# Attention 1: causal masking of the value-side scores moved from TensorE to GpSimd, and the denominators of the fifth block summed on TensorE

## The reference, cut to what matters

```python
B, L, D, H, HD, LD = 2, 1024, 128, 16, 64, 32
q = einsum('bld,dhk->blhk', x, Wq);  latent = einsum('bld,dc->blc', x, Wkv_down)
k = einsum('blc,chk->blhk', latent, Wk_up);  v = einsum('blc,chk->blhk', latent, Wv_up)
attn = einsum('bqhd,bkhd->bhqk', q, k) / sqrt(HD)
mask = arange(L)[None, :] <= arange(L)[:, None]
attn = softmax(where(mask, attn, neg_inf), axis=-1)
y = einsum('bhqk,bkhd->bqhd', attn, v);  out = x + einsum('bqhd,hdo->bqo', y, Wout)
```

## Time and profile before

| | before |
|---|---|
| median of three runs | 2079.44 us |
| profiled execution, its own time | 2081.13 us |
| its span, first to last instruction | 2079.3 us |
| TensorE busy | 1822.3 us (88%) |
| VectorE (DVE) busy | 1597.8 us (77%) |
| ScalarE (ACT) busy | 1195.2 us (57%) |
| GpSimd (POOL) busy | 952.4 us (46%) |
| mean granted TensorE clock | 0.951 |

### The profile page before, as it was taken

One profiled execution on the slowest core, in us unless ns is written; L12 is line 12 of the kernel. 1 busy time (PEld: TensorE's weight loads), 2 busy tenths in 40 slices (PEclk: granted clock), 3 DMA queues, 4 the chain that ended last, 5 costly groups with the idle time before them and its releaser, 6 DMA issues.

```text
span 2079.3 us, 33170 instructions
## 1 busy us (share of the span) xinstructions
PE 1822.3 (88%) x12499; PEld 1206.6 (58%) x12499; DVE 1597.8 (77%) x2101; ACT 1195.2 (57%) x2056; POOL 952.4 (46%) x384
## 2 busy tenths in 40 slices
PE   6899999986889976999999888899887777999998
PEld 4444454355445665767777555556554555677776
DVE  4566656448779978577776899899999999777666
ACT  2354544533878821546555677777777666555554
POOL 3366556512387822010000288888989899300000
PEclk9799999998999987999999999999999999999999
DMA  3111211000222210001100000000001000101000
GB/s 87 32 32 32 58 32 37 1 12 0 74 81 82 102 36 16 20 32 31 31 16 1 1 2 2 1 1 1 2 1 32 1 2 2 46 16 31 16 16 21
DMA packets 39555, 53.98 MB, mean 26 GB/s; under 512 B 6179, under 2 KB 22790, under 8 KB 39398
## 3 DMA queue, kind: packets, MB, share of 16 engines
q1 hardware_dynamic: 38870, 50.82, 8.6%
q10 hardware_dynamic: 528, 1.05, 0.2%
HBM read 37.83 MB, written 1.18 MB: 19 GB/s over the span
## 4 chain that ended last, share of the span: by engine, by line
PE 53%; DVE 18%; issue 17%; POOL 5%; ACT 4%; DMA 1%; SPq 1%; DVEq 0%; ACTq 0%; POOLq 0%; PEldq 0%
PE ps L46 10%; PE ps L48 8%; PE ps L47 8%; DVE negm L2708 7%; PE ps L1690 5%; PE ps L532 3%; PE ps L548 3%; PE ps L1678 2%; PE ps L581 2%; DVE AF L2715 2%; PE ps L573 2%; POOL AR_plain L2513 1%; PE ps L2537 1%; PE ps L2620 1%; PE ps L938 1%
## 5 line engine op out<-in xcount | busy, mean ns | idle before, releaser
L2708 DVE TENSOR_REDUCE negm<-ps 128x64 bf16<-128x1024 f32 x256 | 301.5, 1210 | 20.2 <-PE ps L2611 20.1
L2513 POOL TENSOR_TENSOR AR_plain<-AF 128x2048 f32<-128x2048 f32 x64 | 261.9, 4097 | 31.4 <-ACT AF L2664 31.3
L2672 ACT ACTIVATE AF<-ps 128x1024 f32<-128x1024 f32 x192 | 196.4, 1023 | 133.7 <-PE ps L2620 132.3
L46 PE MATMUL ps<-XH,AR 128*128 128x512 f32 x616 | 255.9, 415 | 14.7 <-DVE XL L251 4.0
L755 POOL TENSOR_TENSOR AF<-AF 128x2048 f32<-128x2048 f32 (+3 forms) x52 | 184.7, 3552 | 177.7 <-ACT AF L695 174.8
L48 PE MATMUL ps<-XH,AR 128*128 128x512 f32 x616 | 246.3, 400 | 0.0
L47 PE MATMUL ps<-XL,AR 128*128 128x512 f32 x616 | 245.9, 399 | 0.0
L695 ACT ACTIVATE AF<-ps 128x512 f32<-128x512 f32 (+1 forms) x304 | 154.0, 576 | 146.1 <-PE ps L532 67.8
L2620 PE MATMUL ps<-negm,ident_bf 128*128 128x512 bf16 x512 | 161.4, 398 | 80.5 <-DVE negm L2708 80.1
L2715 DVE TENSOR_REDUCE AF<-AF 128x128 f32<-128x2048 f32 x96 | 218.2, 2273 | 0.0
L285 POOL TENSOR_SCALAR var_eps<-mv 128x8 f32<-128x8 f32 x10 | 4.2, 422 | 377.6 <-DVE mv L262 377.6
(11 more groups left out here) (329 smaller groups left out, 4238.9 us busy)
## 6 DMA issues: line engine op xcount, KB each, us to landing
AF<-scan_c_rows SPq DMA_DIRECT2D x32, 512.0 KB, 3.6
AR<-AR SPq DMA_DIRECT2D x96, 128.0 KB, 2.4
AF<-in_L_ffn_Wg_dram SPq DMA_DIRECT2D x21, 256.0 KB, 2.6
AF<-in_L_ffn_Wu_dram SPq DMA_DIRECT2D x21, 256.0 KB, 3.0
AF<-in_L_ffn_Wd_dram SPq DMA_DIRECT2D x21, 256.0 KB, 3.7
AF<-in_L_attn_a_Wq_dram SPq DMA_DIRECT2D x1, 512.0 KB, 4.1
AF<-in_L_attn_a_Wout_dram SPq DMA_DIRECT2D x1, 512.0 KB, 8.7
lnt<-in_L_ffn_W_fc_dram SPq DMA_DIRECT2D x2, 256.0 KB, 6.7
```

The costliest lines, as they stand in the source:

```text
L46: pe.matmul(out, ah, bh, start=start, stop=False)
L2513: pool.tensor_tensor(p6[m % 3].rearrange("p (j q i) -> p j q i", j=HJ, i=2), e6[m % 4].rearrange("p (j q i) -> p j q i", j=HJ, i=2), w6i[: ...
L2672: act.activation(o[:, :, q0:q0 + 2 * SUB], bank(2 * (j % 3), 2).rearrange("p (j c) -> p j c", j=HJ), ACT.Exp).then_inc(s6_e, 1)
L2708: dve.tensor_reduce(negm6[:, j % 4, :], bank(2 * (j % 3), 2).rearrange("p (j q i) -> p q j i", j=HJ, i=2), mybir.AxisListType.XY, ALU.max, ...
```

## The change

The scores are no longer masked by TensorE. Behind the exponentials of a diagonal step, GpSimd sets the entries above the diagonal to zero, by one `affine_select` over 128 partitions and 4 heads times 128 columns, in place. `values(t)` also waits for the masks up to step t (a new semaphore `s0_mk`), and so do the additions on GpSimd and, instead of the exponentials, "z". The mask of step t stands in GpSimd's stream ahead of the addition of step t. `late` begins at `n` = 4, so that GpSimd no longer adds the fifth block of `c` = 1 and TensorE sums it inside "z". The tile `causalT_bf` and the two instructions that made it go.

```diff
-        causalT_bf = tf(P // 2).bitcast(BF16)
+        s0_mk = sem("s0_mk")
         def late(t):
             gg, c, n = STEPS[t]
-            return c == 1 and n >= 5 and (gg, c) != PE_SUMS
+            return c == 1 and n >= 4 and (gg, c) != PE_SUMS
+        def masked(t):
+            gg, c, n = STEPS[t]
+            return n >= 4 * c
+            # MASKS_TO[t]: number of masked steps before step t
             # scores(t, j)
                 ins = pe.matmul(o, kst[:, gg // G0, P * n:P * n + P], qst[gg % 2][:, c, h0:h0 + nh_, c0:512],
                                 start=True, stop=True)
-                if n >= 4 * c:
-                    ins = pe.matmul(o[:, :, 0:P], ident_bf[:, :], causalT_bf.unsqueeze(1).to_broadcast([P, nh_, P]),
-                                    start=False, stop=True, skip_group_check=True)
             # values(t)
                 pe.wait_ge(s0_e, SLOT_OF[t + 1])
+                pe.wait_ge(s0_mk, MASKS_TO[t + 1])
             # item "z"
-                    last = [t for t in range(LAST[u] - 2, LAST[u] + 1) if late(t)]
+                    last = [t for t in range(LAST[u] - 3, LAST[u] + 1) if late(t)]
                     if last:
-                        pe.wait_ge(s0_e, SLOT_OF[LAST[u] + 1])
+                        pe.wait_ge(s0_mk, MASKS_TO[LAST[u] + 1])
             # s0_pool, at the head of each step
+                if masked(t):
+                    pool.wait_ge(s0_e, SLOT_OF[t + 1])
+                    block = (zacc[u % 2] if n == 0 else pt[t % 4])[:, :, 0:P]
+                    pool.affine_select(out=block, in_=block, compare_op=ALU.is_ge, fill=0.0, base=0,
+                                       pattern=[[0, 4], [1, P]], channel_multiplier=-1).then_inc(s0_mk, 1)
                 if pooled(t):
                     pool.wait_ge(s0_e, SLOT_OF[t + 1])
+                    pool.wait_ge(s0_mk, MASKS_TO[t + 1])
             # constants, on GpSimd
-            link(pool.memset(causalT_bf, 0.0))
-            link(pool.affine_select(out=causalT_bf, in_=causalT_bf, compare_op=ALU.is_ge, fill=MASKED,
-                                    base=0, pattern=[[1, P]], channel_multiplier=-1))
```

More of the change, by code:

```diff
@@ L397, in late @@
             gg, c, n = STEPS[t]
-            return c == 1 and n >= 5 and (gg, c) != PE_SUMS
+            return c == 1 and n >= 4 and (gg, c) != PE_SUMS
         def pooled(t):
             return STEPS[t][2] > 0 and STEPS[t][:2] != PE_SUMS and not late(t)
-        SLOT_OF, ADDS_TO = [0], [0]
+        def masked(t):
+            gg, c, n = STEPS[t]
+            return n >= 4 * c
+        SLOT_OF, ADDS_TO, MASKS_TO = [0], [0], [0]
         for t in range(N_STEP):
+            MASKS_TO.append(MASKS_TO[-1] + (1 if masked(t) else 0))
             SLOT_OF.append(SLOT_OF[-1] + len(slots(t)))
```

## The result

The changed kernel takes 2152.45 us in the median of six runs (2147.51 to 2159.38); the kernel before takes 2080.12 in six. The ratio is 1.0349, 95% interval [1.0333, 1.0365]: 72 us slower, against a forecast of 2153. The profiled execution is the shortest of the six, 2147.51 us with a span of 2145.8.

What follows compares the result with a forecast made beforehand. The prediction took stage 0 to be bound by TensorE, which would now wait on GpSimd's queue. Waits of 50 us plus 24 for the lowered clock, on 2081.13, gave 2155, forecast as 2153 us; range 2113 to 2190.

Steps and rivals of the forecast that it cites:

- The wait in c = 1: Second chunk of a regular stage-0 group: `values` of n = 4 waits for its mask behind GpSimd's additions, 5.25 us later.
- The wait in c = 0: First chunk of a group: `values` of n = 3 waits behind GpSimd's masks, additions and product, 2.7 us later.
- First and last group: Waits at stage 0's ends: 2.3 us in the first group; 1.9 plus about 1 in the last.
- The clock: TensorE's granted clock falls after the new waits: 2.5 us per long one, 1 per short one, 24 us in all.
- Between the waits: Rest of each group: mask savings against a longer "z" and new mask waits; 0 taken, ends -0.7 and +1.06 us.
- the masks taken off TensorE: From `values` of c = 1, n = 4 to the next group, ahead of "z": removed masks save 1.7 us a group.
- the pricing of a removed matmul by the spacing of starts: Stage 0's 176 mask matmuls, priced by how far apart matmuls start: 27 us of TensorE time removed.
- the opening reading: Stage 0 is bound by TensorE, busy 41.59 of 44 us in the fourth group; GpSimd runs behind it without harm.
- The dear mask: Rival: GpSimd masks take 1.28 us each, 28 of them on the path, 18 us more: 2171 us; chance 0.14.
- The faster rival: GpSimd fits the masks in, no `values` waits, and stage 0 ends 20 us sooner: 2059 us; chance 0.04.

## Why the prediction was right

*The wait in c = 1* was sized at 15.8 us from the first addition to `values` of n = 4. From the end of the exponential, some 0.07 us earlier, it is 15.79 to 15.81 us in five groups and 18.30 in the fifth group, 2.2 more than before, as worked out. Over the six middle groups the third piece grew by 28.3 us; the terms had given 5 x 5.25 + 2.2 = 28.5.

*The wait in c = 0* was sized at 2.7 us. It is 2.9: a step of 0.14 us between a mask's end and the addition behind it (242.03 to 242.17) was left out. Over the six groups 17.2 us instead of 16.2.

*First and last group*: 3.2 and 3.5 us against 2.3 and 2.9, the clock included. With the two waits above this makes 52 us, where 50 were forecast. The 3.2 is partly chance: the profiled execution of the kernel before ended the exponentials of the first group's n = 1 at 74.56 us, that of the changed kernel at 70.93. Counted from there the first group grew by 6.9 us; one trace each can't tell how much of that the change made.

The waits that the trace records, 61.1 us, are more than these pieces grew. TensorE, rid of its mask matmuls, has less to do ahead of them (in the fourth group 5.29 us busy in the first piece instead of 5.73, 9.70 in the third instead of 9.96).

*The clock* was oversized: 24 us forecast, 18 to 19 by the run with added matmuls as measured, some 21 with what those matmuls cost by themselves. The second pieces of the six groups, behind the short waits, lost 6.5 us together, about 1 each as I had put it, but two of them lost nothing and one lost 2.5. The fourth pieces, behind the long ones, lost 1.5 to 2.3 us against the run with added matmuls (21.55 - 20.08 = 1.5 in the fourth group), 11.7 in the six, where I had 2.5 each. (Of the seven long waits that I called about 5 us, my own sum had two at 3.3 and 2.2.) Whether a lower clock follows a short wait differs from group to group.

*Between the waits* I took 0 a group, with +1.06 as the upper end. With the clock at 1.00 the fourth piece is 20.08 us instead of 19.55: +0.5 a group, 2.7 us in the six middle groups. Two mis-sized terms are in it: "z" costs 0.9 instead of 1.06, and the masks taken off TensorE return at most 0.6 there instead of 1.7. The step that failed is the pricing of a removed matmul by the spacing of starts. It gives TensorE's time and not the path's; the run without masks got back 6.5 us of 27. So the opening reading, that the stage is bound by TensorE since it is busy 41.59 of 44 us, holds only in part.

In the six middle groups the waits make 45.5 us, the clock 18.2 and the rest 2.7; with 6.7 for the first and last group that is 73 us, by which the end of stage 0 moved. The oversized clock and the undersized remainder nearly cancelled, so the time was hit more closely than the terms deserve.

*The dear mask* is excluded by 0.634 us in the median, 0.62 having been taken. The figure of 769 ns in the Trainium skill ("GPSIMD Engine Reference", section "Elementwise — side-by-side cycle accounting") is above what the trace shows for this instruction at this size; the measurement decides. *The faster rival* had its deciding point right, since the mask came 5.2 us late there, and its price wrong: the run without any mask shows that 20 us were never to be had.

## What to carry to other kernels

Before a wait is put on an engine with a low busy share, read what will stand in its queue at that moment: here GpSimd was idle for over 10 us in every group, and still 5 us late where it was asked. Put the instruction that another engine waits for ahead of work that only has to be done by the end, and move a step to a slower engine only where its consumer already comes later than that engine needs. A removed instruction is worth what the path gives back, and leaving it out of a kernel for one run measures that at once.

## What was not expected of the hardware

In the kernel before, TensorE was busy 59.98 of the 60 us from 1100 on, and its granted clock there was 0.94; in the changed kernel the corresponding stretch, 59.97 us busy of 60, has 1.00. By stretches of 5 us the clock was 1.00 up to 1125, then 0.81, 0.84 and 0.66, and 1.00 again from 1140; TensorE is recorded busy for all 5.00 us of each stretch from 1090 to 1140. So the clock fell once without any idle time that these records show; its cause stays open.

```profile
1100.00:1160.00 60.00, 59.98 (x235) 43.84 (x235) 36.44 (x53) 31.72 (x55) 0.00 (x0) 0.94 0.00 1
```

```profile
1173.00:1233.00 60.00, 59.97 (x249) 44.07 (x249) 38.29 (x56) 35.21 (x59) 0.00 (x0) 1.00 0.00 1
```
